# Layer 0's first four experts get their rows by products, and the answers come back batch by batch

## What is computed

```python
x = x + _L0_xattn_ref(_layernorm(x, axis=-1), ctx_1024, mask_BxS2_ik0, ...)
x = x + _L0_ffn_ref(_layernorm(x, axis=-1), ...)
x = x + _L1_xattn_ref(_layernorm(x, axis=-1), ctx_1024, ...)
...
x = x + _L3_ffn_ref(_layernorm(x, axis=-1), ...)
```

## Time and profile before

| | us |
|---|---|
| median of 3 runs | 1168.15 (1166.42 to 1169.07) |
| the profiled execution's own time | 1169.73 |
| its span in the profile | 1167.9 |
| from the slots to the first turn of an expert's rows | 249.8 to 274.2 |
| from there to the end of the last output | 274.2 to 324.3 |
| from there to the last group of gathered answers | 324.3 to 348.6 |

### The profile page before, as it was taken

The page is one execution under the profiler, slowest core; times in us unless marked ns, Lnnn a source line. Parts: engine busy times, 40 slices in busy tenths (PEclk is TensorE's granted clock), DMA queues, the critical chain, the costliest instruction groups (busy, mean ns, idle before and its releaser), DMA issues. The chain is left out here.

```text
span 1167.9 us, 15202 instructions
## 1 busy us (share of the span) xinstructions
PE 928.1 (79%) x5428; PEld 624.8 (53%) x5433; DVE 564.4 (48%) x1251; ACT 439.4 (38%) x769; POOL 238.6 (20%) x274
## 2 busy tenths in 40 slices
PE   6886699634746629999876968999699988879998
PEld 4663345324634416777745952223256676747776
DVE  5875446253226471211656758676154447731111
ACT  2341446432322104334343323676432233433443
POOL 0551301034053100000354542201000012320110
PEclk9995979857977857999888996999899989978999
DMA  8014410313620000111000032410001110000111
GB/s 334 1 37 100 129 30 19 137 63 108 187 79 1 1 0 1 37 37 35 1 1 1 1 91 46 123 42 3 1 27 30 38 37 1 1 1 19 37 37 37
DMA packets 33263, 55.68 MB, mean 48 GB/s; under 512 B 3697, under 2 KB 25398, under 8 KB 32817
## 3 DMA queue, kind: packets, MB, share of 16 engines
q1 hardware_dynamic: 32176, 52.86, 14.8%
q0 software_dynamic: 1024, 1.98, 0.6%
HBM read 44.79 MB, written 9.96 MB: 47 GB/s over the span
## 5 line engine op out<-in xcount | busy, mean ns | idle before, releaser
L2302 PE MATMUL psum<-xT_all,wexp 128*128 128x512 f32 x400 | 184.3, 606 | 1.2 <-issue 0.7
L1505 DVE TENSOR_REDUCE arena<-psum 128x2 f32<-128x1024 f32 (+3 forms) x128 | 127.2, 1021 | 79.6 <-PE psum L2088 49.9
L1047 ACT ACTIVATE arena<-psum 128x512 f32<-128x512 f32 (+3 forms) x256 | 116.0, 515 | 85.8 <-PE psum L2101 48.3
L740 POOL TENSOR_TENSOR rstd<-var,held 128x8 f32<-128x8 f32 (+3 forms) x22 | 46.1, 2116 | 384.6 <-DVE var L1258 358.2
L2302 PEld LDWEIGHTS psum<-xT_all,wexp 128*128 128x128 f32 x400 | 74.4, 195 | 78.6 <-issue 73.6
L2317 PEld LDWEIGHTS psum<-wexp,arena 128*128 128x128 f32 x800 | 95.9, 195 | 14.9 <-issue 14.8
L2085 PE MATMUL psum<-arena 72*128 72x512 bf16 (+3 forms) x256 | 82.6, 394 | 25.6 <-DMA arena<-parts_q 12.4
L2013 PE MATMUL psum<-values_out_all,arena 128*128 128x128 f32 x560 | 77.3, 286 | 26.6 <-ACT arena L1011 26.5
L2317 PE MATMUL psum<-wexp,arena 128*128 128x128 f32 x800 | 96.2, 278 | 0.0
L815 POOL TENSOR_TENSOR arena<-arena,small 128x616 f32<-128x616 f32 x56 | 67.9, 1215 | 126.4 <-DVE small L1435 126.2
L2013 PEld LDWEIGHTS psum<-values_out_all,arena 128*128 128x128 f32 x560 | 68.1, 194 | 36.3 <-ACT arena L1011 34.9
(11 more groups left out here) (292 smaller groups left out, 1400.0 us busy)
## 6 DMA issues: line engine op xcount, KB each, us to landing
wexp<-experts SPq DMA_DIRECT2D x24, 514.0 KB, 3.6
parts_k<-wexp SPq DMA_DIRECT2D x12, 384.0 KB, 2.9
arena<-parts_k SPq DMA_DIRECT2D x48, 96.0 KB
arena<-parts_q SPq DMA_DIRECT2D x48, 96.0 KB
arena<-experts SPq DMA_DIRECT2D x8, 514.0 KB, 3.7
arena<-rows SPq DMA_DIRECT2D x8, 512.0 KB, 8.8
wexp<-experts SPq DMA_DIRECT2D x9, 384.0 KB, 3.1
held<-packed SPq DMA_DIRECT2D x1, 2375.0 KB, 15.6
```

Of the source, the lines that this page charges most:

```text
L740: pool.tensor_tensor(dst, src, half[0:src.shape[0], 0:n], ALU.pow).then_inc(done, 1)
L1047: act.activation(p_self[:, n % 2, kt % 2, j, lo:S], bank(t_bank("keys", c, k), lo, S), ACT.Exp, scale=DS ** -0.5).then_inc(ut_ok, 1)
L1505: dve.tensor_reduce(top[:, x % 2, qt, j:j + 2], src, AX_X, ALU.max, negate=True).then_inc(us_ok, 1)
L2302: mm(bank(c, 0, BANK), wexp[:, side, c * P:(c + 1) * P], xT_all[:, b * S:(b + 1) * S], start=True, stop=True).then_inc(h_ps, 1)
```

## The change

Four things are changed. The first four experts no longer read their rows from `queued`: VectorE compares each token's place in the expert's queue (`ranks`) with the numbers 1 to 128 (`places`, 128 new columns among the constants) and so writes a selection matrix for each of the 8 tiles (`selected`, line 1844 of the new kernel), and TensorE gets the turned rows as the sum of 8 products of `xn_moe` with it (`queue`, line 2397). All 16 scatters stay. SP asks for the rows of experts 4 to 7 together, when the scatters are done. Gates, bias products and bias addition move behind the experts' stage, the norm sums and `inverse_norms` too, and ACT's squares ahead of it. And the gathers come in the order of `returns()`: both choices of batch 0, then both of batch 1. Behind each batch its four statistics are taken, so that layer 1 begins with their combination (`known=True`).

```diff
+        "places": np.broadcast_to(np.arange(1, P + 1, dtype=f), (P, P)),
...
+        ranks, row_sums = M["diag"][:, 0:P], M["diag"][:, P:P + 64]
+        chosen = [D["back"][:, n * 1024:(n + 1) * 1024] for n in range(2)]
...
-            for e in range(-max(ahead for _, ahead in lagged), 0):
+            for e in range(-max(ahead for _, ahead in lagged), 4):
                 steps(e, e, 0)
-            with eng.Fori(0, E0 // 4 - 1) as i:
+            with eng.Fori(0, E0 // 4 - 2) as i:
                 for k in range(4):
-                    steps(i * 4 + k, k, i)
+                    steps(i * 4 + (4 + k), k, i + 1)
...
+        def returns():
+            return [(2 * b + k, k * NT + b * TB + t) for b in range(B) for k in range(2) for t in range(TB)]
...
-            sp.wait_ge(scattered, 16 * 16)
-            for side in range(4):
-                load_queue(side, side)
...
+            for e in range(4):
+                if e == 2:
+                    sp.wait_ge(scattered, 16 * 16)
+                    for side in range(4):
+                        load_queue(4 + side, side)
+                sp.wait_ge(d_O, e + 1)
+                load0(e + 4, e)
+                store_answer(e, e)
...
-                inverse_norms()
...
-                for n in range(2 * NT):
+                for g, n in returns():
...
                 elif l == 1:
+                    inverse_norms()
...
+                if l == 0:
+                    for e in range(8):
+                        act.wait_ge(n_in, 16 * 8)
+                        act.activation(rows3[:, e, :], rows3[:, e, :], ACT.Square).then_inc(n_sq, 1)
+                    return
...
                     dve.tensor_copy(slot_i[:, 0:16], to).then_inc(slots_ok, 1)
...
+                    step.then(dve.tensor_tensor(M["pre"], bank(0, 0, 2 * n), M["mk"], ALU.mult))
+                    step.then(dve.tensor_tensor(ranks, M["pre"][:, 0:n], M["pre"][:, n:2 * n], ALU.add))
+                    return
...
+                def selected(e, side, i):
+
+                    if not isinstance(e, int) or e > 3:
+                        return
+                    if e > 1:
+                        dve.wait_ge(d_T, e - 1)
+                    dve.tensor_tensor(chosen[side % 2].rearrange("p (t c) -> p t c", c=P),
+                                      w("places").unsqueeze(1).broadcast_to([P, NT, P]),
+                                      ranks.rearrange("p (t e) -> p t e", e=E0)[:, :, bass.ds(e, 1)].broadcast_to([P, NT, P]),
+                                      ALU.is_equal).then_inc(d_hot, 1)
+
+                run_queues(dve, (selected, 3), (features, 2), (answer, 0))
+                gates0()
+                own_values(1)
...
+                add_biases(0)
+                for g in range(2 * B):
+                    dve.wait_ge(d_back[g], 16 * 4)
+                    for n in [n for group, n in returns() if group == g]:
...
+                    step.then(last)
+                    if g % 2:
+                        last = measured(x_res, range(g // 2 * TB, g // 2 * TB + TB))
...
+                def queue(e, side, i):
+
+                    if not isinstance(e, int) or e > 3:
+                        pe.wait_ge(d_in[side], i * 16)
+                        pe.wait_ge(d_xe, e + 1)
+                        turn(bank(side % 2, 0, P), D["xin"][:, side * P:(side + 1) * P], ident).then_inc(d_T, 1)
+                        return
+                    pe.wait_ge(d_hot, e + 1)
                     pe.wait_ge(d_xe, e + 1)
-                    turn(bank(side % 2, 0, P), D["xin"][:, side * P:(side + 1) * P], ident).then_inc(d_T, 1)
+                    for t in range(NT):
+                        last = mm(bank(side % 2, 0, P), xn_moe[:, t * P:(t + 1) * P], chosen[side % 2][:, t * P:(t + 1) * P],
+                                  start=(t == 0), stop=(t == NT - 1))
+                    last.then_inc(d_T, 1)
...
-                run_queues(pe, (turned, 2), (hidden, 1), (output, 0))
+                run_queues(pe, (queue, 2), (hidden, 1), (output, 0))
                 prep(1)
+                biases(0)
```

More of the change, by code:

```diff
@@ L1192, in activate @@
                     last.then_inc(d_h, 1)
-                for e in range(8):
-                    act.wait_ge(n_in, 16 * 8)
-                    act.activation(rows3[:, e, :], rows3[:, e, :], ACT.Square).then_inc(n_sq, 1)
                 act.preload_act_table(ACT.Gelu)
@@ L1242, in carry, with measured, moments @@
                 dve.memset(small[:, j, 63:64], 0.0)
-            def moments(src, done, rms=False, eps=EPS_LN, tiles=range(NT)):
-                lo, hi = tiles[0], tiles[-1] + 1
+            def measured(src, tiles):
                 for t in tiles:
                     last = dve.bn_stats(stats[:, t, :], src[:, t * P:(t + 1) * P])
-                step.then(last)
+                return last
+            def moments(src, done, rms=False, eps=EPS_LN, tiles=range(NT), known=False):
+                lo, hi = tiles[0], tiles[-1] + 1
+                if not known:
+                    step.then(measured(src, tiles))
                 for t in tiles:
@@ L1361, in xattn @@
                 held_in(dve, [0, 2, 3, 4][l])
-                moments(x_res, x_stat)
+                moments(x_res, x_stat, known=(l == 1))
                 if l == 2:
@@ L1806, in experts0 @@
                 dve.tensor_scalar(s2_col, s2_col, 1e-24, None, ALU.max).then_inc(n_max, 1)
[L1807 to L1816 removed]
+                add_biases(0)
+                for g in range(2 * B):
+                    dve.wait_ge(d_back[g], 16 * 4)
+                    for n in [n for group, n in returns() if group == g]:
+                        a = x_res[:, n % NT * P:(n % NT + 1) * P]
+                        last = dve.scalar_tensor_tensor(a, D["back"][:, n * P:(n + 1) * P], D["slot"][:, 48 + n:49 + n], a,
+                                                        ALU.mult, ALU.add)
+                    step.then(last)
+                    if g % 2:
+                        last = measured(x_res, range(g // 2 * TB, g // 2 * TB + TB))
                 last.then_inc(d_done, 1)
@@ L2272, in gating, with biases @@
                        start=False, stop=True, skip_group_check=True).then_inc(g_loc, 1)
-                if l != 2:
-                    n = [1, 2, 0, 3][l]
-                    pe.wait_ge(gate_ok, n)
-                    for t in range(NT):
-                        last = turn(psum[0:E_, GB[l] * BANK + t * P:GB[l] * BANK + (t + 1) * P], gates[:, t, 0:E_], ident)
-                    last.then_inc(gT_ps, 1)
-                    pe.wait_ge(gT_ok, n)
-                    for t in range(NT):
-                        last = mm(psum[:, BB[l] * BANK + t * P:BB[l] * BANK + (t + 1) * P], gatesT[0:E_, t * P:(t + 1) * P],
-                                  w(f"m{l}_b2"), start=True, stop=True)
-                    last.then_inc(b2_ps, 1)
-                    if l == 0:
-                        pe.wait_ge(b2_ok, n)
+                elif l != 2:
+                    biases(l)
+            def biases(l):
+                E_ = MOE[l]["E"]
+                n = [1, 2, 0, 3][l]
+                pe.wait_ge(gate_ok, n)
+                for t in range(NT):
+                    last = turn(psum[0:E_, GB[l] * BANK + t * P:GB[l] * BANK + (t + 1) * P], gates[:, t, 0:E_], ident)
+                last.then_inc(gT_ps, 1)
+                pe.wait_ge(gT_ok, n)
+                for t in range(NT):
+                    last = mm(psum[:, BB[l] * BANK + t * P:BB[l] * BANK + (t + 1) * P], gatesT[0:E_, t * P:(t + 1) * P],
+                              w(f"m{l}_b2"), start=True, stop=True)
+                last.then_inc(b2_ps, 1)
+                if l == 0:
+                    pe.wait_ge(b2_ok, n)
             def experts(l):
```

80 lines of the change are left out of this document (42 added, 38 removed).

## The result

| | before | after |
|---|---|---|
| median of 5 runs, us | 1168.15 (1166.42 to 1169.07) | 1174.39 (1173.44 to 1176.53) |
| ratio, 95% interval | | 1.0059 [1.0038, 1.0079] |

What follows compares the result with a forecast made beforehand. Layer 0's experts were taken to start only when GpSimd's 16 scatters are done, with layer 1 behind the gathers. −9.8 − 0.8 + 0.2 = −10.4 us gave 1157.8 us against the median 1168.15; range 1154.5 to 1161.5.

Steps and rivals of the forecast that it cites:

- End of the stage: Return behind the last output (its end is T): moved work covered by gathers landing at T + 24.4, by at least 1.2 us.
- a new chain at the end: Rival, 6%: in the return, VectorE's sums and biases outlast the gathers by up to 2 us, up to 1159.8 us.
- Front of the stage: First four experts' selections and 52 products before turn(4): 16 to 17.3 us, over at 268 to 269, before the scatters end.
- the front is too slow: Rival, 8%: TensorE stays at the lower clock in the front, which ends 4.3 us after the scatters, 1162.1 us.
- The stall that stays: TensorE at turn(4) still waits for the 16 scatters: resumes at about 274.2 instead of 284.20, 10.0 us earlier.
- Two-input operations beside scatters: VectorE's four selections beside GpSimd's scatters: at most 0.9 us of delay, taken as nothing.
- the rival at 4.9: Rival, 10%: each of four selections holds GpSimd's scatters for its whole 1.22 us, turn(4) 4.9 us later, 1162.7 us.
- The clock at the resumption, and turn(8): From turn(4): lower clock until 278.7, costing 2.25 us; turn(8), 4.0 us behind output(4), at 287.1 instead of 296.70.
- Sum of the stage: Last output of the experts' stage 9.8 us earlier, at 314.5, with bounds 8.1 and 12.0.
- Statistics: Four of eight statistics done before the last group of gathers lands: 0.8 us gained behind it.
- Packing: 128 more columns in the constants' transfer at the start: costs 0 to 0.6 us, taken as 0.2.
- The norm sums: VectorE's 9.10 us of sums moved into the return, covered by the gathers; VectorE free for the bias addition at T + 15.

Runs made afterwards that it cites:

- e18: The changed kernel again, in job 5, on a chip without late signals: 1162.34 us, ratio 0.9943 to the kernel before.
- e7: The changed kernel with GpSimd's 16 scatters replaced by 16 plain transfers from SP, in job 2: 1154.31 us, ratio 0.9869 to before.
- e2: The kernel before with only the 128 new columns among the constants: 1167.72 us, ratio 0.9978 to before.
- e10: The changed kernel with gates and biases inside the experts' stage and SP waiting for the scatters one step earlier, in job 3: 1168.19 us, ratio 0.9989 to before.
- e9: The changed kernel again, in job 3: 1176.29 us, ratio 1.0071 to before.
- e3: The changed kernel with the first four experts' rows by transfers, as before: 1183.47 us, ratio 1.0113 to before.
- e1: The changed kernel again, for a second trace, in job 1: 1186.4 us, one run.
- e12: The changed kernel again, as the control of job 4: 1176.73 us, ratio 1.0079 to before.
- e20: The kernel before with only the gathers batch by batch and the statistics per batch, in job 5: 1166.35 us, ratio 0.9978 to before.
- e5: The kernel before with only the gathers batch by batch and the statistics per batch, in job 2: 1165.96 us, ratio 0.9969 to before.
- The first job: The job that ran e1 to e4, with the kernel before beside them: 1186.4, 1167.72, 1183.47 and 1175.49 us.
- e6: The changed kernel with GpSimd's 16 gathers replaced by 16 plain transfers from SP, in job 2: 1153.00 us, ratio 0.9858 to before.
- e8: The changed kernel with gates and biases inside the experts' stage and SP waiting for the scatters one step earlier, in job 2: 1162.72 us, ratio 0.9966 to before.
- e19: The changed kernel with gates and biases inside the experts' stage and SP waiting for the scatters one step earlier, in job 5: 1162.49 us, ratio 0.9941 to before.
- e13: The changed kernel with plain SP transfers instead of the 16 gathers, indirect scatters kept, in job 4: 1161.79 us, ratio 0.9948 to before.
- e4: The changed kernel with the eight norm sums moved behind the answers of experts 0 and 1, four each: 1175.49 us, ratio 1.0038 to before.
- e14: The changed kernel with plain SP transfers instead of the 16 scatters, indirect gathers kept, in job 4: 1164.37 us, ratio 0.9959 to before.

## Why the prediction was wrong, step by step

**End of the stage: the step that failed.** "So the biases are there at T + 14.9 (full clock) to T + 17.7" and "so all of it is covered". On the chips without late signals they were there at T + 15.2 and T + 15.3 (e18, e7). On the others, wherever the gathers were GpSimd's, it was T + 27.3 to T + 31.1, past the cover of T + 24.4. The sum had −0.8 us for the whole return and it became +9.8. In after the addition began at T + 29.4, 5.0 us behind that cover, and all additions of answers stood behind it. The rival "a new chain at the end" named this place, at up to 2 us and by VectorE's work; VectorE had waited 14.74 us for the bias products. The trace of before did not show it: it has ACT waiting for TensorE beside the gathers, on time, where e2 has the same waits late. I took times that one trace showed beside the transfers as the kernel's own, with at least 1.2 us of cover behind them; where signals are late the biases come 12 to 16 us later.

**Front of the stage.** Forecast 16 to 17.3 us. Without late signals it was 13.7 us (e18). Two terms were too high. TensorE's clock rose about 3.8 us behind the first product instead of 4.5 to 7 (granted 0.50 from 252 to 256, 0.68 from 256 to 257, 1.00 from 257 to 266), which by my prices would give 15.6 us. And I priced four products by the length of their row, 1.06 us, while such rows overlap: hidden(3) starts at 264.57 and output(1) at 265.46 in e18, 0.89 us for four. The front was slack in any case. With late signals the front took 23.2 us. The rival "the front is too slow" named this size, but for another reason: the granted clock was high (0.99 below) while the results were late. Stretches of after, columns as in the earlier trace rows:

```profile
252.00:262.00 10.00, 9.56 (x82) 9.18 (x81) 3.50 (x5) 1.67 (x7) 7.56 (x9) 0.99 0.13 46
...
286.00:290.00 4.00, 0.49 (x2) 0.47 (x3) 0.10 (x1) 0.00 (x0) 0.00 (x0) 0.96 0.90 286
290.00:293.00 3.00, 3.00 (x15) 3.00 (x15) 0.31 (x1) 1.14 (x4) 0.00 (x0) 0.50 0.11 35
```

**The stall that stays: "the stage resumes at turn(4) at about 274.2".** It takes in only TensorE's queue. SP's wait for the scatters stands behind its wait for output(1), and the slow front reached that: rows asked for at 272.55, 3.3 us behind the end of the last scatter. With SP's wait one place earlier turn(4) is at 25.9 us instead of 29.3 in the same job (e10, e9). My sum took SP's order only together with a front that ends in time. (In e18 it ends in time, and turn(4) is at 25.8 us.)

**Two-input operations beside scatters.** I took 0 and kept 0.9 us as the bound, with the rival at 4.9. It was 1.4: the scatters took 21.8 us in e18 (251.87 to 273.67) and 20.4 without selections (e3, and 250.76 to 271.11 before). The first scatter took 2.00 us beside the first two selections instead of 1.20, and a later one 1.54 instead of 0.97; a scatter beside the third selection (256.74, beside 257.00 to 258.22 in e18) took 0.97 as ever. All 11 traces with selections and scatters have 21.2 to 22.4 us, all 6 without selections 20.3 to 20.4. The Trainium skill (SBUF — State Buffer, "Who interferes with whom") says that a VectorE operation with two SBUF inputs contends with a GpSimd instruction that reads SBUF, and infers that writing descriptors does not suffer. I took the first half for the operation's full length. The traces agree with neither reading: four selections of 1.2 us held the scatters for 1.4 us in all, more than nothing and less than the full 4.9.

**The clock at the resumption, and turn(8).** The lower level at turn(4) came as forecast. From turn(4) to turn(8) I had 12.9 us; the changed kernel's traces have 12.7 to 14.2. In e18 output(4) ends 7.7 us behind turn(4), where I had 8.9, but turn(8) then starts 6.4 us behind output(4) (284.40 to 290.85) instead of 4.0. The rows are asked for at 285.12 and take 5.7 us; before it was 3.3 (293.39 to 296.70). Steps without waits ask for the weights of four experts, 514 KB each, within 6.1 us (280.59 to 286.69), and the DMA engines are 0.90 busy at 280 GB/s from 287 to 291 (before: 0.63 at 188 GB/s from 292 to 296). That this is what delays the rows was not tested. What I also missed is the next fall of the clock: TensorE waits 3.93 us (e18: 4.34) for turn(8) where it waited 1.38 to 1.70 before, and the products behind that are at the lower level again (0.50 in the last row above). (In e1 2.33 us of waiting were followed by the lower level, in e12 2.64 us were not.) From turn(8) to the last output it was 29.2 us in e18 and 27.6 before.

**Sum of the stage.** Forecast −9.8 us at the last output. e18 has −5.3 (69.2 against 74.5): 1.4 for the scatters, 1.3 up to turn(8), 1.6 behind it, and the 0.2 that I had added for odd experts. So on a chip without late signals too this term was nearly twice the measured one, and the time 6.3 us below before instead of 10.4.

**Statistics: right.** −0.8 forecast; from the last output to the combination 26.6 us (e20) against 27.3. **Packing: right**, no cost to be seen (e2). **The norm sums: right**, they cost nothing in the return: in e18 VectorE is ready for the biases at T + 14.7, T + 15 was forecast, and waits 0.53 us for TensorE.

**What stays open.** In 6 of 17 traces with indirect gathers the first gather begins 4.4 to 4.9 us behind the last output, in the others 2.7 to 2.8, in kernels of both kinds (e5 and e20 are one kernel, e20 has 2.8). It explains why e18's statistics come at 28.7 us instead of 26.6. Why some chips have late signals isn't settled, nor whether it goes with the chip or with the hour, since no chip was used twice. The first job's chips aren't on record. No kernel without the 128 new columns was traced where signals are late; the columns alone aren't the cause (e6 to e8, e18 and e19 have them). Whether TensorE's results themselves are late or only the signals is open too, since the ends of its rows are modelled. In e13 and e12 the rows of the front have no gaps and end where e18's do (13.7 and 13.8 us behind the first product), and in e13 the granted clock has fallen to 0.50 by 269, as behind the front of e18, 5 us before output(1)'s signal is taken at 274.17: this speaks for finished work with a late signal. In after, e1, e4, e9 and e10 TensorE's own later products of the front also come with gaps in which it waits for nothing that the profile shows. That only work of TensorE was waited for behind "remote" holds in every trace.

## What to carry to other kernels

Before you move necessary work into a stretch that another engine's transfers cover, look in that stretch for who waits for this engine today, and look in traces from more than one chip: here one trace had such waits end on time and another had waits of up to 6.4 us in their place, and a cover of a few us was not enough. Follow the resumption through every queue that has to ask for something, also for the case that the part ahead is slow. Where steps come closer together, so do the transfers that they ask for: price them anew. And run a close call on more than one chip: the same kernel was 0.6 to 0.8% slower in three jobs and 0.6% faster in another.

## What the runs showed of the hardware that was not expected

On some chips, results of TensorE reach VectorE, ACT and SP up to 12 us late while GpSimd issues indirect transfers at one every 1.25 to 1.28 us (the gates' turns of after end at 331.85 and are copied at 343.64). The last of them come 0.3 us (return of after) to 2.4 us (fronts) behind the end of the last transfer's issue. With plain transfers from SP in their place they are on time on the same chip (e12 to e14). On two of the five chips of the experiments nothing was late beside the same indirect transfers (e5 to e8, e18 to e20). The granted clock stays high in the front while it happens (0.99 from 252 to 262 in after). The mark that all these traces share is a wait of the consumer that ended by "remote"; gaps between TensorE's own products stand beside it in five of the seven late fronts, and in e12 and e13 not.
